# Negated row maxima carried in the query stack of an attention stage, in place of a product of their own

## The chip, the cores and the metric

One core of a Trainium2 chip runs the whole kernel in one launch. The metric is the device time of a launch in microseconds, the median of three runs. A profiled execution gives the trace; its own time stands beside its span below.

## The reference

A block of three parts over x of 8 batches x 256 tokens x 256 columns: a mixture-of-experts layer at half weight, attention, and the same experts again. The attention between them, on a layer-normed x, is

```python
q, k, v = (proj(w_q), proj(w_k), proj(w_v))          # 16 heads of 16
scores = jnp.einsum('bhqd,bhkd->bhqk', q, k) * SCALE
probs = jax.nn.softmax(scores, axis=-1)
attn = jnp.einsum('bhqk,bhkd->bhqd', probs, v)
return jnp.einsum('bsd,ed->bse', attn.transpose(0, 2, 1, 3).reshape(b, s, d), w_o)
```

## The kernel before, in words

The first stage routes the tokens and runs the first experts, the `attention` function does attention and the routing of the second experts, then come the second experts and the sum. Each engine has one program, written out by hand; semaphores tie them. `s_x` in the code is a semaphore, `wait_ge` waits for its count, `then_inc` counts at an instruction's end. DMAs count 16 at their landing.

**Split numbers.** TensorE multiplies in fp32r, so q and k are kept as a high and a low part. The two *stacks*, `qs` and `ks` (three buffers each, `NST`), hold for each of 8 head pairs 64 rows per head: row 4d + r of a half of the partitions is dim d in part r. The query stack has parts high, low, high, low and the key stack high, high, low, low, so that one 64-row matmul gives all four products of parts. `stack_heads` (L1291) fills row r of every four with one DMA of 256 KB from `qk`, issued on SyncE's queue (L1309 to L1314); for batch 0 ScalarE issues two of the key's.

**Attention, steps.** `cycle` (L1281) runs every engine's `step(b, j)` for b from -1 to 7 and j from 0 to 7; step j handles head pair j of batch b and, through `lagged` (L1287), the scores by key of the pair that is five steps (`LAG`) older: j = 5 has pair 0 of the same batch, j = 0 has pair 3 of the batch before.
- `scores` (L1453, TensorE): scores by query into `psS`; VectorE takes their negated maxima over the keys (`maximum`, L1723), one `tensor_reduce` of 1.2 us.
- After pairs 3 and 7, `split_maxima` (L1734) splits four pairs' maxima into high and low, TensorE's `maxima` (L1502) turns them (two transposes into `psG[1]`), and ScalarE's `maxima` (L1984) copies them to `nmT`: 8 rows per head parity (4 pairs high, then 4 low), 256 queries wide.
- `scores_by_key` (L1467): the pick product first, which adds to each score of pair j its query's negated maximum: `pick` is a matrix of zeros and ones that takes the high and low row of pair j out of `nmT`. Then the products of the stacks, keys by queries, on top of it. ScalarE takes the exponential of 1024 columns (`exponentials`, L1992), and `values` (L1487) multiplies by v.
- Between these stand projections of the next batch (`project`, `project_v`), the output's transposes and product (`by_query`, `by_dim`, `result`) and the routing of three batches before (`rows_turned`, `logits`, `ranks`, `gates_turned`, `biases`); GpSimd sums the partial results of the first experts (`sum_parts`, L1320) and sends routed rows by indirect DMA (`send`, L1350).

TensorE's `step` (L1610) has in step 0 scores, scores by key, `maxima(b - 1, 1)`, `rows_turned`, the projection of q; in step 4 scores, scores by key, `maxima(b, 0)`, `result`. ScalarE's `step` (L2072) has in steps 0 and 4 the exponential first, then the copy of the maxima. The maxima of the first half are first read in step 5, of the second half in step 1 of the next batch.

**SyncE in attention** (L1309): per batch, wait for the scores by key of batch b-3, load the partials of batch b+2 (1 MB), fill the query stack after `s_ql` (VectorE's low part of q, step 1 of the batch before), the key stack after `s_kl` (step 3).

**The pick table** is made in the first stage by GpSimd (`make_pick`, L183), between two inverse roots.

Of the kernel before, what the change touches and what calls it, by code (L numbers as in the profile page):

```python
# [14 lines left out]
P = 128  # L15
# [99 lines left out]
def constants(program, mem, x, x_in, nw, gate_wT, gate_b, b_raw):  # L115
# [20 lines left out]
    c["pick"] = mem.sb("pick", [P, NH // 4, P], fp32r)  # L136
    pick_f, picked = mem.sb("pick_f", [P, NH // 4, P], fp32), mem.sem("picked")
# [22 lines left out]
    def _(pool):  # L160
# [3 lines left out]
                  pool.memset(c["one_e"][:, :], 1.0), pool.memset(pick_f[:, :, :], 0.0)]  # L164
# [18 lines left out]
    def make_pick(pool):  # L183

        ch = Chain(pool, picked)
        for g in range(NH // 4):
            for line in (g, NH // 4 + g, P // 2 + g, P // 2 + NH // 4 + g):
                ch.link(pool.affine_select(out=pick_f[:, g, :], in_=pick_f[:, g, :], compare_op=ALU.not_equal, fill=1.0,
                                           base=-line, pattern=[[0, P]], channel_multiplier=1))
        ch.link(pool.tensor_copy(c["pick"][:, :, :], pick_f[:, :, :]))  # L190

# [4 lines left out]
    return c, (s_x_in, loaded, made, all_there, make_pick)  # L196
# [210 lines left out]
def route(program, nc, m, c, there, x, table, rows, banks, routed, split, b_raw, b_first, first_biases):  # L407
# [8 lines left out]
    s_x_in, loaded, made, all_there, make_pick = there  # L416
# [169 lines left out]
    def _(pool):  # L586
# [5 lines left out]
        make_pick(pool)  # L592
# [593 lines left out]
def attention(program, nc, m, c, x, xn, kbuf, proj, table, rows, psum, routed, early):  # L1186
# [24 lines left out]
    pick = c["pick"]  # L1211
# [57 lines left out]
    s_ld = [m.sem(f"ld{i}") for i in range(NST)]  # L1269
# [129 lines left out]
    def _(pe):  # L1399
# [53 lines left out]
        def scores(b, j):  # L1453
# [4 lines left out]
            if j == 0:  # L1458
                pe.wait_ge(s_ld[i], (b // NST + 1) * 128)
# [7 lines left out]
        def scores_by_key(b, j):  # L1467
# [3 lines left out]
            i, n, g = b % NST, b * HP + j, j % 4  # L1471
            pe.wait_ge(s_nT, n // 4 + 1)
# [5 lines left out]
            for odd in range(2):  # L1478
                rows = slice(odd * HALF, (odd + 1) * HALF)
                pe.matmul(bank[:, odd * 512:(odd + 1) * 512], pick[rows, g, :], nmT[rows, n // 4 % 2, None, :].to_broadcast([HALF, QT, S]), start=True, stop=False)  # L1480
            for k in range(QT):
                for odd in range(2):
                    rows = slice(odd * HALF, (odd + 1) * HALF)
                    last = pe.matmul(bank[:, (odd * QT + k) * S:(odd * QT + k + 1) * S], ks[i][rows, j, k * P:(k + 1) * P], qs[i][rows, j, :], start=False, stop=k == QT - 1)  # L1484
# [125 lines left out]
        def step(b, j):  # L1610
# [3 lines left out]
            scores(b, j)  # L1614
            scores_by_key(*lagged(b, j))
            if j == 0:
                maxima(b - 1, 1)
# [13 lines left out]
            if j == 4:  # L1631
                maxima(b, 0)
# [329 lines left out]
    def _(act):  # L1962
        def high_part(b, which):
# [7 lines left out]
            elif b > 0:  # L1971
                act.wait_ge(s_ld[(b - 1) % NST], 128 * ((b - 1) // NST + 1))
            act.activation(dst[0], src, ACT.Copy, scale=scale).then_inc(s_hi, 1)

        def keep_v(b):
# [3 lines left out]
            act.wait_ge(s_vz, 2)  # L1979
            since(act, s_pv, 4 * (b - 1))  # L1980
# [3 lines left out]
        def maxima(b, half):  # L1984
# [4 lines left out]
            since(act, s_t, 4 * (n - 1))  # L1989
# [82 lines left out]
        def step(b, j):  # L2072
            exponentials(*lagged(b, j))
            if j == 0:
                maxima(b - 1, 1)
# [7 lines left out]
            if j == 2:  # L2083
                high_part(b + 1, "k")
                if b < 0:
                    stack_heads(act, b + 1, "k", range(2, 4))
# [4 lines left out]
            if j == 4:  # L2091
                maxima(b, 0)
# [282 lines left out]
```

## Time and profile before

| | |
|---|---|
| median of 3 runs | 862.64 us (858.92 to 864.11) |
| profiled execution, its own time | 856.83 us |
| its span, first to last instruction | 855.1 us |
| attention stage in it | about 349 to 615 us |
| mean granted clock of TensorE in it | 0.957 |

In rows of a timeline: start in us, duration in us, engine, line, operation, what it writes <- what it reads, shapes, count of instructions merged into the row; in brackets the idle time of the engine before it and what ended that. In rows of groups: busy us, mean ns of one, then idle us before them by what ended it. SPq is SyncE's queue, PEld TensorE's weight loads. Names carry a prefix of their stage, `s_a_` for attention.

### The profile page before, as it was taken

The numbers are of one execution on the slowest core, as the hardware profiler recorded it, in microseconds if no ns is written. First come the engines' busy times: TensorE is split into PE (matmuls) and PEld (weight loads), VectorE is DVE, ScalarE is ACT, GpSimd is POOL, SyncE is SP. The second block draws the span as 40 slices with busy tenths as digits, with TensorE's granted clock in tenths as the row PEclk, the third lists the DMA queues.
The fourth block names the chain that finished last, engine by engine and source line by source line (L and its number), as shares of the span: only waits on it lengthen the run. The fifth ranks groups of instructions, "written<-read, shape, count | busy, mean of one in ns | idle before, by whom it ended". The sixth has DMA issues, their size and how long they took to land.

```text
span 855.1 us, 17528 instructions
## 1 busy us (share of the span) xinstructions
PE 729.3 (85%) x4774; PEld 568.2 (66%) x4774; DVE 602.2 (70%) x1435; ACT 432.6 (51%) x922; POOL 458.0 (54%) x446
## 2 busy tenths in 40 slices
PE   1775649999999997789999889787499999999984
PEld 1443326788888886667766667555268888888872
DVE  4775737777777776477787577457387777777766
ACT  3655324555555555257656455454325555555551
POOL 6876723666666667433344342146516666666672
PEclk9999999999999999999999798689689999999998
DMA  8998878868888753544453223027555787887766
GB/s 303 347 388 333 314 238 319 282 217 281 266 284 294 242 192 117 188 158 162 148 184 120 92 106 121 34 68 262 201 162 184 252 256 258 268 268 242 228 229 227
DMA packets 87419, 188.87 MB, mean 221 GB/s; under 512 B 13072, under 2 KB 37920, under 8 KB 85792
## 3 DMA queue, kind: packets, MB, share of 16 engines
q1 hardware_dynamic: 47104, 106.07, 36.4%
q10 hardware_dynamic: 26448, 41.92, 14.8%
q0 software_dynamic: 13776, 39.75, 12.2%
q8 instruction: 46, 0.75, 0.4%
q14 instruction: 45, 0.37, 0.1%
HBM read 105.46 MB, written 65.45 MB: 200 GB/s over the span
## 4 chain that ended last, share of the span: by engine, by line
PE 35%; DVE 13%; another core or an unknown queue 4%; issue 3%; ACT 2%; POOL 1%; DMA 0%; SPq 0%; DVEq 0%; ACTq 0%
PE s_psT L945 12%; PE s_psG L969 6%; DVE s_a_nm L1732 4%; PE s_psO L1499 3%; PE s_psS L1464 2%; PE s_psS L926 2%; PE s_psS L912 2%; PE s_psG L1436 2%; PE s_psT L1480 1%; DVE all_x L2188 1%; PE s_psT L1484 1%; PE s_psR L1571 1%; PE s_psG L1449 1%; PE s_psG L1522 1%
## 5 line engine op out<-in xcount | busy, mean ns | idle before, releaser
L1357 POOL DMA_INDIRECT rows<-s_a_row,s_a_slot_i x64 | 62.4, 975 | 107.6 <-DVE s_a_slot_i L1860 88.9
L1132 POOL DMA_INDIRECT kbuf<-s_e_own_ys,s_e_own_place x79 | 80.9, 1024 | 66.3 <-ACT s_e_own_ys L1078 58.3
L1132 POOL DMA_INDIRECT kbuf<-f_e_ys,f_e_place x79 | 80.9, 1024 | 66.3 <-ACT f_e_ys L1078 58.6
L945 PE MATMUL f_bank<-f_e_w,f_e_th 128*128 x316 | 114.3, 462 | 2.0 <-ACT f_e_th L1100 1.9
L945 PE MATMUL s_psT<-s_e_own_w,s_e_own_th 128*128 x316 | 112.1, 455 | 1.9 <-SPq L811 0.9
L1732 DVE TENSOR_REDUCE s_a_nm<-s_psS 128x4 f32<-128x1024 f32 x64 | 78.3, 1223 | 50.1 <-PE s_psS L1464 40.5
L1999 ACT ACTIVATE s_a_pT<-s_psT 128x1024 f32<-128x1024 f32 x62 | 63.4, 1022 | 47.0 <-PE s_psT L1484 30.4
L1008 DVE TENSOR_TENSOR s_e_own_hb<-s_psT,s_e_own_bias 128x512 f32<-128x512 f32 x79 | 54.5, 690 | 39.7 <-PE s_psT L945 38.7
L1008 DVE TENSOR_TENSOR f_e_hb<-f_bank,f_e_bias 128x512 f32<-128x512 f32 x79 | 54.5, 690 | 39.1 <-PE f_bank L945 37.2
L603 POOL DMA_INDIRECT rows<-f_r_row,f_r_slot_i x64 | 66.5, 1039 | 27.0 <-issue 18.5
L945 PEld LDWEIGHTS f_bank<-f_e_w,f_e_th 128*128 128x128 f32 x316 | 60.5, 192 | 22.5 <-issue 3.7
L945 PEld LDWEIGHTS s_psT<-s_e_own_w,s_e_own_th 128*128 128x128 f32 x316 | 59.4, 189 | 21.2 <-issue 2.5
L1138 POOL TENSOR_TENSOR f_e_bc<-f_e_bc,f_e_am 128x512 f32<-128x512 f32 x40 | 53.2, 1331 | 25.8 <-DVE f_e_bc L1041 24.9
L1138 POOL TENSOR_TENSOR s_e_own_bc<-s_e_own_bc,s_e_own_am 128x512 f32<-128x512 f32 x40 | 52.1, 1302 | 23.8 <-DVE s_e_own_bc L1041 22.6
L945 PE MATMUL f_bank<-f_e_w,f_e_tl 128*128 x158 | 56.3, 437 | 0.0
L945 PE MATMUL s_psT<-s_e_own_w,s_e_own_tl 128*128 x158 | 55.4, 431 | 0.0
L912 PE MATMUL f_bank<-all_ident,f_e_tb 128*128 128x128 f32 x160 | 43.4, 279 | 10.0 <-DMA f_e_tb<-rows 10.0
L969 PE MATMUL s_psG<-s_e_own_w,s_e_own_ah 128*128 x316 | 50.8, 283 | 0.2 <-issue 0.2
L969 PE MATMUL f_bank<-f_e_w,f_e_ah 128*128 x316 | 50.8, 282 | 0.1
L1078 ACT ACTIVATE s_e_own_ys<-s_psG,s_e_tb 128x256 f32<-128x256 f32 x79 | 37.5, 475 | 22.1 <-PE s_psG L969 21.3
L969 PEld LDWEIGHTS s_psG<-s_e_own_w,s_e_own_ah 128*128 128x128 f32 x316 | 45.6, 188 | 3.6 <-issue 0.4
L969 PEld LDWEIGHTS f_bank<-f_e_w,f_e_ah 128*128 128x128 f32 x316 | 45.6, 188 | 3.4 <-issue 0.3
(383 smaller groups left out, 1887.5 us busy)
## 6 DMA issues: line engine op xcount, KB each, us to landing
w_split<-stage ACTq DMA_DIRECT2D x10, 1536.0 KB
f_e_w<-w_split SPq DMA_DIRECT2D x24, 512.0 KB
s_e_own_w<-w_split SPq DMA_DIRECT2D x24, 512.0 KB
f_e_tb<-rows ACTq DMA_DIRECT2D x80, 144.0 KB
s_e_tb<-rows ACTq DMA_DIRECT2D x80, 144.0 KB
stage<-w_raw SPq DMA_DIRECT2D x11, 768.0 KB
s_a_qs<-s_a_qk SPq DMA_DIRECT2D x32, 256.0 KB, 2.5
s_a_ks<-s_a_qk SPq DMA_DIRECT2D x30, 256.0 KB, 2.5
```

Source lines behind the costliest of these rows:

```text
L603: pool.indirect_dma_start(out=rows[:, :], out_offset=bass.IndirectOffsetOnAxis(ap=slot_i[i][:, t, k:k + 1], axis=0), in_=row[i][:, t, :], ...
L912: last = pe.transpose(psT[:, j, k * P:(k + 1) * P], tb[:, (2 * p + j) % (2 * RING), k * P:(k + 1) * P], c["ident"][:, :])
L945: last = pe.matmul(psH[j][:, :], left[:, p % 2, j, k * P:(k + 1) * P], w1[:, bass.ds(buf, 1), h, k * I2:(k + 1) * I2], start=n == 0, stop= ...
L969: last = pe.matmul(psY[j][:, 0:D], left[:, p % 2, j, k * P:(k + 1) * P], w2[:, bass.ds(buf, 1), h, o:o + D], start=n == 0, stop=n == len(p ...
L1008: dve.tensor_tensor(hb[:, j, :], psH[j][:, :], bias[:, bass.ds(buf, 1), :].rearrange("p a n -> p (a n)"), ALU.add).then_inc(s_hb, 1)
L1078: act.activation(ys[:, n, :], psY[j][:, 0:D], ACT.Copy, scale=tb[:, slot, bass.ds(e + D, 1)]).then_inc(s_ys, 1)
L1132: pool.indirect_dma_start(out=kbuf[:, :], out_offset=bass.IndirectOffsetOnAxis(ap=place[:, n:n + 1], axis=0), in_=ys[:, n, :], in_offset=N ...
L1138: pool.tensor_tensor(bc[:, b, :, :], bc[:, b, :, :], am[:, b, :, :], ALU.mult).then_inc(s_u, 1)
L1357: pool.indirect_dma_start(out=rows[:, :], out_offset=bass.IndirectOffsetOnAxis(ap=slot_i[i][:, t, k:k + 1], axis=0), in_=row[i][:, t, :], ...
L1499: last = pe.matmul(bank[h * VW:(h + 1) * VW, :], vz[:, b % 2, k, 4 * q + h, :], pT[:, (4 * n + h) % 8, k, :], start=k == 0, stop=k == QT - 1)
L1732: dve.tensor_reduce(nm[:, b % 2, :, :, j].rearrange("p t o -> p o t"), src, X_AXIS, ALU.max, negate=True).then_inc(s_mx, 1)
L1999: act.activation(to, score_bank(n)[:, :], ACT.Exp).then_inc(s_e, 1)
```

## The change

The query and the key stack lose their fourth part (low by low). Row 3 of every four is zero instead, except two rows per half: rows 3 and 7, which hold the high and the low of the pair's negated maximum in the query stack and ones in the key stack. So the product of the stacks has the maximum in it, and the pick product, its table and `make_pick` go. Zeros come from the constant `pad`, ones from `vz` before its second half is written; ScalarE therefore waits for those DMAs before it first writes that half. While scores by query of a batch run, the rows of their pairs are still zero.

SyncE takes the rows from `nmT` into the query stack by two DMAs per half batch (`keep_maxima`): those of the first half behind the next batch's key stack, those of the second half at the head of the following round, ahead of the load of partials. Scores by key wait for them (`maxima_kept`) where they waited for ScalarE's copy; the copy waits for the DMAs of two halves before. From batch 3 on the two rows of a query stack are cleared again. TensorE turns the maxima ahead of the scores by key of steps 0 and 4, and ScalarE copies them ahead of the exponential.

```diff
@@ constants, route
-    c["pick"] = mem.sb("pick", [P, NH // 4, P], fp32r)
-    pick_f, picked = mem.sb("pick_f", [P, NH // 4, P], fp32), mem.sem("picked")
...
-        inverse_roots(0, GPT, 1)
-        make_pick(pool)
...
@@ attention
+    def stacked(engine, b):
+
+        engine.wait_ge(s_ld[b % NST], 16 * (4 + 6 + 8 * (b // NST)))
+
+    def key_rows_set(engine, i):
+
+        engine.wait_ge(s_set[i], 16 * 2)
+
+    def max_rows(stack, o):
+
+        return stack[o * HALF + 3:o * HALF + 8:4, :, :].rearrange("p g n -> p (g n)").bitcast(fp32)
+
+    def clear_maxima(queue, b):
+
+        i = b % NST
+        for o in range(2):
+            if b < NST:
+                queue.dma_start(qs[i][o * HALF + 3:(o + 1) * HALF:4, :, :].rearrange("p g n -> p (g n)").bitcast(fp32), c["pad"][:, 0:D]).then_inc(s_ld[i], 16)
+            else:
+                queue.dma_start(max_rows(qs[i], o), c["pad"][0:16, 0:D]).then_inc(s_ld[i], 16)
+
+    def clear_key_rows(queue, i):
+
+        for o in range(2):
+            queue.dma_start(ks[i][o * HALF + 11:(o + 1) * HALF:4, :, :].rearrange("p g n -> p (g n)").bitcast(fp32), c["pad"][0:112, 0:D]).then_inc(s_ld[i], 16)
+
+    def set_key_rows(queue, i):
+
+        for o in range(2):
+            queue.dma_start(max_rows(ks[i], o), vz[0:4, 1, :, :, :].rearrange("p t h w -> p (t h w)")).then_inc(s_set[i], 16)
+
+    def keep_maxima(queue, b, half):
+
+        n = 2 * b + half
+        queue.wait_ge(s_nT, n + 1)
+        for o in range(2):
+            to = qs[b % NST][o * HALF + 3:o * HALF + 8:4, 4 * half:4 * half + 4, :].rearrange("p g n -> p (g n)")
+            queue.dma_start(to.bitcast(fp32), nmT[o * HALF:o * HALF + 8, n % 2, :].bitcast(fp32)).then_inc(s_nq[n % 2], 16)
+
+    def maxima_kept(engine, n):
+
+        engine.wait_ge(s_nq[n % 2], 32 * (n // 2 + 1))
+
-    def stack_heads(queue, b, which, some=range(4)):
+    def stack_heads(queue, b, which, some=range(3)):
...
-        k, s_part, stack, parts = {"q": (0, s_ql, qs[i], (0, 1, 0, 1)), "k": (1, s_kl, ks[i], (0, 0, 1, 1))}[which]
+        k, s_part, stack, parts = {"q": (0, s_ql, qs[i], (0, 1, 0)), "k": (1, s_kl, ks[i], (0, 0, 1))}[which]
...
@@ sync
         for b in range(B):
+            if b >= 2:
+                keep_maxima(sp, b - 2, 1)
             since(sp, s_t, (b - NST + 1) * HP)
             if b + 2 < B:
                 load_parts(b + 2)
+            if b == 0:
+                clear_maxima(sp, 0)
+                clear_key_rows(sp, 0)
+                sp.wait_ge(s_vz, 2)
+                set_key_rows(sp, 0)
+            if b >= NST:
+                clear_maxima(sp, b)
             stack_heads(sp, b, "q")
-            stack_heads(sp, b, "k", range(2 if b == 0 else 4))
+            stack_heads(sp, b, "k", range(2 if b == 0 else 3))
+            if b == 0:
+                for i in range(1, NST):
+                    clear_maxima(sp, i)
+                    clear_key_rows(sp, i)
+                    set_key_rows(sp, i)
+            if b >= 1:
+                keep_maxima(sp, b - 1, 0)
+        keep_maxima(sp, B - 2, 1)
+        for half in range(2):
+            keep_maxima(sp, B - 1, half)
@@ tensor
             if j == 0:
-                pe.wait_ge(s_ld[i], (b // NST + 1) * 128)
+                stacked(pe, b)
+                if b < NST:
+                    key_rows_set(pe, b)
...
-            pe.wait_ge(s_nT, n // 4 + 1)
+            maxima_kept(pe, n // 4)
...
-            for odd in range(2):
-                rows = slice(odd * HALF, (odd + 1) * HALF)
-                pe.matmul(bank[:, odd * 512:(odd + 1) * 512], pick[rows, g, :], nmT[rows, n // 4 % 2, None, :].to_broadcast([HALF, QT, S]), start=True, stop=False)
...
             scores(b, j)
+            if j == 0:
+                maxima(b - 1, 1)
+            if j == 4:
+                maxima(b, 0)
             scores_by_key(*lagged(b, j))
...
@@ scalar
             act.wait_ge(s_nt, n + 1)
-            since(act, s_t, 4 * (n - 1))
+            if n >= 2:
+                maxima_kept(act, n - 2)
             act.activation(nmT[:, n % 2, :], psG[1][:, 0:S], ACT.Copy).then_inc(s_nT, 1)
...
+            if j == 0:
+                maxima(b - 1, 1)
+            if j == 4:
+                maxima(b, 0)
             exponentials(*lagged(b, j))
```

## Rows read from the trace of the kernel before

**Rows 1.** Page: busy us, share of the span and instructions of each engine

```profile
PE 729.3 (85%) x4774; PEld 568.2 (66%) x4774; DVE 602.2 (70%) x1435; ACT 432.6 (51%) x922; POOL 458.0 (54%) x446
```

**Rows 2.** Windows of batches 1, 4, 5: us, PE, PEld, DVE, ACT, POOL busy, PEclk, DMA share, GB/s

```profile
379.00:399.00 20.00, 18.88 (x202) 13.96 (x198) 14.72 (x28) 14.02 (x22) 5.64 (x4) 1.00 0.44 159
...
443.50:472.50 29.00, 25.17 (x239) 18.53 (x235) 21.32 (x60) 16.73 (x30) 14.51 (x13) 0.94 0.31 114
472.50:503.40 30.90, 27.23 (x239) 20.62 (x235) 21.43 (x61) 16.93 (x30) 9.62 (x10) 0.83 0.29 107
```

**Rows 3.** Timeline, first maxima of batches 2 and 4, steps 4 to 6

```profile
410.01 2.48 SPq L1298 DMA_DIRECT2D s_a_ks<-s_a_qk  x4
...
410.99 0.38 ACT L1990 ACTIVATE s_a_nmT<-s_psG 128x256 fp32r<-128x256 f32 x1
...
412.10 0.40 PE L1480 MATMUL s_psT<-s_a_nmT,all_pick 64*128 64x512 f32 x2
412.33 0.40 PE L1484 MATMUL s_psT<-s_a_qs,s_a_ks 64*128 64x256 f32 x4
...
415.45 0.50 PE L1464 MATMUL s_psS<-s_a_ks,s_a_qs 64*128 64x256 f32 x4
...
461.83 2.48 SPq L1298 DMA_DIRECT2D s_a_ks<-s_a_qk  x4
...
463.94 0.40 PE L1480 MATMUL s_psT<-s_a_nmT,all_pick 64*128 64x512 f32 x2
```

**Rows 4.** Timeline, second maxima of batch 2, steps 0 and 1 of batch 3

```profile
420.96 0.44 PE L1510 MATMUL s_psG<-all_ident,s_a_nmx 128*128 128x128 f32 x2
...
421.98 0.38 ACT L1990 ACTIVATE s_a_nmT<-s_psG 128x256 fp32r<-128x256 f32 x1
...
423.53 0.40 PE L1480 MATMUL s_psT<-s_a_nmT,all_pick 64*128 64x512 f32 x2
```

**Rows 5.** Timeline, second maxima of batch 4, the late signals

```profile
476.60 0.96 POOL L1357 DMA_INDIRECT rows<-s_a_row,s_a_slot_i  x1 [0.30 <-issue]
...
478.65 1.02 ACT L1999 ACTIVATE s_a_pT<-s_psT 128x1024 f32<-128x1024 f32 x1 [3.86 <-remote]
...
480.00 0.80 PE L1480 MATMUL s_psT<-s_a_nmT,all_pick 64*128 64x512 f32 x2 [2.40 <-ACT s_a_nmT L1990]
...
480.59 0.63 PE L1484 MATMUL s_psT<-s_a_qs,s_a_ks 64*128 64x256 f32 x4
```

**Rows 6.** Groups of instructions: scores, pick products, transposes of the maxima

```profile
L1464 PE MATMUL s_psS<-s_a_ks,s_a_qs 64*128 64x256 f32 x256 | 33.6, 342 | 12.7 <-DVE s_a_nm L1732 9.2 <-issue 3.3
...
L1480 PE MATMUL s_psT<-s_a_nmT,all_pick 64*128 64x512 f32 x124 | 28.4, 452 | 8.3 <-ACT s_a_nmT L1990 8.0 <-issue 0.2
...
L1510 PE MATMUL s_psG<-all_ident,s_a_nmx 128*128 128x128 f32 x32 | 6.9, 298 | 1.0 <-DVE s_a_at L1761 1.0
```

**Rows 7.** Landings by line: the stacks' 256 KB (L1298), partials' 1 MB (L1307), output stores (L2166)

```profile
DMA to landing us min/median/max: 2.3/2.5/4.4
...
DMA to landing us min/median/max: 5.3/5.4/5.6
...
DMA to landing us min/median/max: 2.0/2.6/3.5
```

**Rows 8.** Timeline, first maxima of batches 1 and 7, steps 4 and 5

```profile
389.72 2.48 SPq L1298 DMA_DIRECT2D s_a_ks<-s_a_qk  x4
...
391.29 0.39 PE L1480 MATMUL s_psT<-s_a_nmT,all_pick 64*128 64x512 f32 x2
...
554.92 0.38 ACT L1990 ACTIVATE s_a_nmT<-s_psG 128x256 fp32r<-128x256 f32 x1
...
556.02 0.40 PE L1480 MATMUL s_psT<-s_a_nmT,all_pick 64*128 64x512 f32 x2
```

**Rows 9.** Timeline, first stage, the second inverse root and its reader

```profile
14.32 2.28 POOL L590 TENSOR_TENSOR f_r_root<-f_r_var,all_minus_half 128x12 f32<-128x12 f32 x1
...
19.58 0.16 DVE L495 TENSOR_SCALAR f_r_gain<-f_r_root 128x6 f32<-128x6 f32 x1
```

More of the change, by code:

```diff
@@ L163, in _ @@
                   pool.memset(c["zero"][:, :], 0.0), pool.memset(c["spare"][:, :], 0.0), pool.memset(c["minus_half"][:, :], -0.5),
-                  pool.memset(c["one_e"][:, :], 1.0), pool.memset(pick_f[:, :, :], 0.0)]
+                  pool.memset(c["one_e"][:, :], 1.0)]
         for f in filled:
@@ L181, in _ @@
         pool.iota(c["places"][:, :, :], pattern=[[GPT * P, NG], [1, GPT]], base=-T, channel_multiplier=GPT, **approx).then_inc(made, 1)
[L183 to L190, printed above, removed]
     def all_there(engine, gates=True):
@@ L195, in all_there @@
         engine.wait_ge(made, 11 if gates else 10)
-    return c, (s_x_in, loaded, made, all_there, make_pick)
+    return c, (s_x_in, loaded, made, all_there)
 class Chain:
@@ L407, in route @@
 def route(program, nc, m, c, there, x, table, rows, banks, routed, split, b_raw, b_first, first_biases):
-    s_x_in, loaded, made, all_there, make_pick = there
+    s_x_in, loaded, made, all_there = there
     TT = NG * GPT
@@ L1210, in attention @@
     nmT = m.sb("nmT", [P, 2, S], fp32r)
-    pick = c["pick"]
     nmx = m.sb("nmx", [P, 2, QT, P], fp32)
@@ L1268, in attention @@
         "var", "rstd", "xn", "xT", "xh", "xl", "q", "qh", "ql", "k", "kh", "kl", "vp", "vv"))
-    s_ld = [m.sem(f"ld{i}") for i in range(NST)]
+    s_ld, s_nq = [m.sem(f"ld{i}") for i in range(NST)], [m.sem(f"nq{i}") for i in range(2)]
+    s_set = [m.sem(f"set{i}") for i in range(NST)]
     (s_s, s_mx, s_nh, s_nl, s_nt, s_nT, s_t, s_e, s_pv, s_o, s_on, s_rd, s_at, s_aT, s_ah, s_al, s_f, s_x) = (m.sem(n) for n in (
@@ L1470, in scores_by_key @@
                 return
-            i, n, g = b % NST, b * HP + j, j % 4
-            pe.wait_ge(s_nT, n // 4 + 1)
+            i, n = b % NST, b * HP + j
+            maxima_kept(pe, n // 4)
             bank = score_bank(n)
@@ L1483, in scores_by_key @@
                     rows = slice(odd * HALF, (odd + 1) * HALF)
-                    last = pe.matmul(bank[:, (odd * QT + k) * S:(odd * QT + k + 1) * S], ks[i][rows, j, k * P:(k + 1) * P], qs[i][rows, j, :], start=False, stop=k == QT - 1)
+                    last = pe.matmul(bank[:, (odd * QT + k) * S:(odd * QT + k + 1) * S], ks[i][rows, j, k * P:(k + 1) * P], qs[i][rows, j, :], start=True, stop=True)
             last.then_inc(s_t, 1)
@@ L1614, in step @@
             scores(b, j)
+            if j == 0:
+                maxima(b - 1, 1)
+            if j == 4:
+                maxima(b, 0)
             scores_by_key(*lagged(b, j))
             if j == 0:
-                maxima(b - 1, 1)
                 rows_turned(b - 3)
@@ L1631, in step @@
             if j == 4:
-                maxima(b, 0)
                 result(b - 2)
@@ L1971, in high_part @@
             elif b > 0:
-                act.wait_ge(s_ld[(b - 1) % NST], 128 * ((b - 1) // NST + 1))
+                stacked(act, b - 1)
             act.activation(dst[0], src, ACT.Copy, scale=scale).then_inc(s_hi, 1)
@@ L1979, in keep_v @@
             act.wait_ge(s_vz, 2)
+            if b == 1:
+                for n in range(NST):
+                    key_rows_set(act, n)
             since(act, s_pv, 4 * (b - 1))
@@ L2072, in step @@
         def step(b, j):
+            if j == 0:
+                maxima(b - 1, 1)
+            if j == 4:
+                maxima(b, 0)
             exponentials(*lagged(b, j))
             if j == 0:
-                maxima(b - 1, 1)
                 routed_turned(b - 3)
@@ L2085, in step @@
                 if b < 0:
-                    stack_heads(act, b + 1, "k", range(2, 4))
+                    stack_heads(act, b + 1, "k", range(2, 3))
                 routed_residual(b - 3)
@@ L2091, in step @@
             if j == 4:
-                maxima(b, 0)
                 if b >= 0:
```

## The prediction

> **What bounds the kernel now.** The profile page comes first, for scale: TensorE has records for 85% of the span, VectorE for 70% [rows 1]. Then the table of windows, cut at each batch's first scores. Batches 1, 4 and 5 of the attention stage take 20, 29.0 and 30.9 us. In batch 1 TensorE's records cover 18.9 us and VectorE has 5 to spare; in 4 and 5 TensorE has nearly 4 us without a record, and the clock is granted at 0.94 and 0.83 [rows 2]. So in the early batches the order written for TensorE sets the pace, and in the later ones a hole is added to it.
>
> The timeline shows the two places that the change touches. A batch has eight steps, and the scores by key run five steps later. The first maxima (heads 0 to 3) are turned in step 4 and first read in step 5; the second are turned in step 0 of the next batch and first read in its step 1. In batch 2 ScalarE's copy of the first ends at 410.99 + 0.38 = 411.37, and the pick product that reads it starts at 412.10: 0.7 us of slack [rows 3]. The copy of the second ends at 422.36 and is read at 423.53: 1.2 us [rows 4]. In batch 4 it is another picture: TensorE, idle for 2.40 us, reads the copy at 480.00, at the slow clock (the two picks take 0.80 where they took 0.40). ScalarE had waited to 478.65 for a signal that the view can't name, while GpSimd issued indirect DMAs one behind the other until 477.56 [rows 5]. Over the stage the wait for this copy is 8.0 us of TensorE's time [rows 6].
>
> **The change part by part.** All sums stand against the profiled execution: 856.83 us around a span of 855.1. It lies 5.8 us below the median of the three runs, 862.64; I come back to that at the end.
>
> *The pick products go.* Two 512-column matmuls in two row halves side by side: from the first pick to the first product is 412.33 - 412.10 = 0.23 us at the full clock [rows 3], 0.59 at the slow one [rows 5]. 64 steps x 0.23 = 14.7 us is the most at full clock. 16 of the steps are first reads, where the arrival of the maxima will set the start (below); they gain nothing. Of the other 48 (11.0 us) some gain nothing either, because the next scores wait for VectorE's maximum: 9.2 us of such waits today [rows 6]. I take 8, the slow clock's share included; bounds 5 and 15.
>
> *The low parts' products go.* They were row 3 of each four in the same 64-row matmuls, so no matmul gets shorter. Per batch SyncE has two copies of 256 KB fewer; four take it 2.48 us, so 0.62 each [rows 3].
>
> *The maxima take a DMA more.* This is the term that decides. After ScalarE's copy SyncE issues two small DMAs into the query stack, and TensorE waits for both. The trace has none like them. Nearest are the stack's own copies: 0.62 us to issue one, and 2.3 to 2.5 us from issue to landing, with 256 KB in each [rows 7]. Four follow at 0.62 us each and still land in 2.5, so at most 0.6 of that is bytes, which puts a small one between 2.3 - 0.6 = 1.7 and 2.5; the stores of the output land in 2.0 at best [rows 7]. I take 2.1, near those stores, and 0.5 for the issue ahead of it: 2.6 us from a free SyncE to both rows in place; bounds 2.1 and 3.2.
>
> "DMA: Bandwidth & Descriptors" of the Trainium skill (section Anatomy of one DMA) gives any DMA a fixed part of about 2.0 us, most of it the confirmation of the last write, with HBM the heaviest target. By it an estimate for this pair, which stays in SBUF, is 2.5 us at most, and the sum below would be 1 to 2 us less. The stores' row, to HBM, agrees at 2.0.
>
> *First half.* SyncE's program puts this pair behind the next batch's key stack. Those copies start at 410.01, when VectorE's low part is there, and three of them (one fewer than now) hold SyncE until 411.87; the maxima are ready at 411.4 or earlier and wait for it. 411.87 + 2.6 = 414.5 stands against a read at 412.10: 2.4 us. In batch 4, 461.83 + 1.86 + 2.6 = 466.3 against 463.94: 2.35 [rows 3]. In batch 1 the copies start at 389.72 and the read is at 391.29: 2.9. Batch 7 has no next stack: the copy ends at 555.30, some 0.6 earlier in the new order, and 554.7 + 2.6 = 557.3 stands against 556.02: 1.3 [rows 8]. Over eight batches 2 x 2.9 (batches 0, 1) + 5 x 2.35 + 1.3 = 18.9. Behind the waiting product on TensorE stand the values, a transpose and the 12 products that project v, and then the next scores, today at 415.45 [rows 3]. VectorE and ScalarE have one operation each in hand and run dry. Nothing fills the hole, so I count it whole.
>
> *Second half.* Here SyncE stands waiting, so only 2.6 us count, and the copy comes earlier: the transposes go ahead of one scores by key, the copy ahead of one exponential. Batch 2: transposes at about 420.5 in place of 420.96, copy done at 421.2, rows at 423.8 against 423.53: 0.3 [rows 4]. Where the signal comes late, ScalarE copies first, at 478.65, and is done at 479.05: rows at 481.65 against 480.00, 1.65 [rows 5]; 0.5 to 1.65, as TensorE now comes there later anyhow; I take 1.3 for each of the four late batches (3 to 6). Batches 0 and 1 have a read that follows the copy more closely, 0.9 each; the last, with a short tail behind it, 1.4: 1.8 + 0.3 + 5.2 + 1.4 = 8.7.
>
> *The transposes ahead.* They wait for VectorE's split and normalise, 1.0 us in all today with a scores-by-key group in front of them as cover [rows 6]. That group (0.23 us without its picks) now stands behind the wait: between 0 and 0.25 per half, 16 x 0.125 = 2.
>
> *The clock.* Waits of 2.3 to 2.9 us are new in TensorE. Batch 1 keeps the full clock with 1.1 us in all without a record [rows 2]; behind the 2.40 us before 480.00 it runs at half [rows 5]. Bounds: nothing, and the half clock behind each of eight waits. At half clock a step of about 2.5 us of TensorE work loses as much again: 8 x 2.5 = 20. I take 4: the wait is a single one, where the one before 480.00 had late signals ahead of it.
>
> *SyncE's other DMAs.* The load of partials for two batches on stood behind the key stack and now stands behind the second maxima, in batch 2 at about 422.5. It takes 5.4 us [rows 7], so GpSimd can sum from 428, and the statistics of it are due at the head of batch 4, 443.50 [rows 2]: cover 10 us even with a sum of 5, cost 0. The clears stand ahead of the query stack, which has six steps. In the prologue six small copies stand ahead of the first query stack, of which four overlap its wait; two cost 1 us, and two fewer stack copies give it back. The twelve behind delay only a load. 0, within 1 either way.
>
> *GpSimd's pick table goes.* Without it the second root of the first stage, at 14.32, could start up to 0.7 earlier. VectorE reads it at 19.58 only, behind its own queue [rows 9]: 3 us of cover, cost 0.
>
> Sum: -8 + 18.9 + 8.7 + 2 + 4 = +25.6; 856.8 + 25.6 = 882.4 for a profile like this one, and with a part of the 5.8 us to the median, 884.
>
> **The rivals.** (1) *Faster.* The small rows land in 1.7 us, SyncE issues them in 0.3, and the earlier transposes take away the 8.0 us of waiting; 14.7 + 8 = 23 of gain stands against first waits of 1.1 us, 8 x 1.1 = 9: 857 - 14 = 843. For it: 18.9 of 20 us in batch 1 are TensorE's. Against it: three key copies hold SyncE whatever a landing takes. (2) *Absorbed.* The waits of step 5 are had back in the later batches, because the late signals end with GpSimd's burst and not with TensorE's work: 5 x 2.35 = 11.8 less, and 5 less from the second half. 25.6 - 16.8 = +9: 866. Against it: the signals come one at a time there, so a step less is done when the burst ends. (3) *Slower still.* The clock falls behind every first wait, +16: 900. It fell in batches 4 and 5 [rows 2].
> That the change doesn't do what it says isn't likely to show in the time: the maxima must be in the stack before the read, whatever their values.
>
> **How the numbers follow.** Forecast 0.62, (1) 0.10, (2) 0.13, (3) 0.15. The forecast's own bounds: landing and issue move 15 waits by 0.5 each, -8 to +9, and the picks' gain is 5 to 15: 868 to 895. The range reaches into (2) and (3): 861 to 902. Faster 0.10 is (1); within 1% (854 to 871, about what a measurement of this kernel tells from no change) 0.12 is most of (2) and the forecast's edge; slower 0.78.
>
> **What would show it.** Right: the picks gone; in step 5 of every batch an idle TensorE of 2 to 3 us before the scores by key, ended by a DMA into the query stack; the row pair issued right behind three key copies; batch 1 at about 23 us where it was 20. The stages before and after unchanged within 1 us. Wrong: if step 5 shows no hole, I misread the landing or SyncE's order; if the hole is there and the batches aren't longer, something absorbed it, and I'd look in the stretch of late signals.

## The result and the profile after

| | before | after |
|---|---|---|
| median | 863.38 us (4 runs, 858.92 to 864.14) | 884.41 us (4 runs, 881.21 to 890.40) |
| ratio, 95% interval | | 1.027, 1.0226 to 1.0313: slower |
| profiled execution, its span | 856.83, 855.1 us | 890.40, 888.7 us |
| mean granted clock in it | 0.957 | 0.936 |

884.0 was forecast and 884.4 came out. A ratio with its interval is estimated from runs set beside one another; it isn't the quotient of the two medians (here 1.024) and can lie some tenths of a per cent from it. The profiled execution of after is the longest of its four, 6 us over their median, and that of before lies 6.5 us under its own. The two differ by 33.6 us where the medians differ by 21.0, so what they show is read as parts of a loss that is some 12.6 us too large.

The page's busy line and the group of the scores by key, of after; [rows 1] and [rows 6] are the ones of before that answer to them:

```profile
PE 737.0 (83%) x4646; PEld 569.4 (64%) x4646; DVE 607.5 (68%) x1435; ACT 433.2 (49%) x922; POOL 451.3 (51%) x428
...
L1533 PE MATMUL s_psT<-s_a_qs,s_a_ks 64*128 64x256 f32 x248 | 31.9, 340 | 22.4 <-DMA s_a_qs<-s_a_nmT 22.4
```

TensorE has 128 instructions fewer and is 7.7 us longer busy: the instructions that are left take longer, at a lower granted clock. The group shows the new wait: 22.4 us of an idle TensorE, ended by the maxima's DMA. The very last half is computed in another bank, `s_psS`, and waits 1.2 us more.

Batch 1 of after, step 4 to the scores of step 6, from the timeline:

```profile
399.11 0.41 PE L1559 MATMUL s_psG<-all_ident,s_a_nmx 128*128 128x128 f32 x2 [1.20 <-DVE s_a_at L1812]
...
399.55 0.38 ACT L2045 ACTIVATE s_a_nmT<-s_psG 128x256 fp32r<-128x256 f32 x1 [1.63 <-PE s_psG L1559]
399.58 1.82 SPq L1329 DMA_DIRECT2D s_a_ks<-s_a_qk  x3
400.82 0.50 PE L1516 MATMUL s_psS<-s_a_ks,s_a_qs 64*128 64x256 f32 x4 [0.86 <-DVE s_a_nm L1783]
401.45 1.36 SPq L1316 DMA_DIRECT2D s_a_qs<-s_a_nmT  x2
403.99 0.80 PE L1533 MATMUL s_psT<-s_a_qs,s_a_ks 64*128 64x256 f32 x4 [2.67 <-DMA s_a_qs<-s_a_nmT]
404.71 1.93 PE L1548 MATMUL s_psO<-s_a_pT,s_a_vz 128*32 128x256 f32 x16
...
406.92 2.91 PE L1499 MATMUL s_psG<-all_wp,s_a_xp 128*128 128x256 f32 x12
409.76 0.57 PE L1516 MATMUL s_psS<-s_a_ks,s_a_qs 64*128 64x256 f32 x4
```

The copy of the maxima is done at 399.93. SyncE issues the three key copies until 401.40, then the pair until 402.81; TensorE has the rows at 403.99, after 2.67 us of nothing. Behind the wait its work runs at half clock: the 16 value products take 1.93 us, the projection of v 2.91. The trace of the first experiment below, without the pair, has the same two at 1.07 and 1.68. Two shorter waits for VectorE, 1.20 and 0.86 us, stand ahead of the long one.

A hole of nearly the same kind in batch 4 leaves the clock alone. TensorE had no wait of 0.2 us or more in the 7 us ahead of it, and the value products behind it take their 1.07 us:

```profile
492.39 0.50 PE L1533 MATMUL s_psT<-s_a_qs,s_a_ks 64*128 64x256 f32 x4 [1.99 <-DMA s_a_qs<-s_a_nmT]
492.82 1.07 PE L1548 MATMUL s_psO<-s_a_pT,s_a_vz 128*32 128x256 f32 x16
```

Then the attention stage as a whole, from the first scores to the last scores by key, and batches 1, 4 and 5 in it. Windows: us, busy time of PE, PEld, DVE, ACT, POOL, PEclk, DMA share, GB/s. Before:

```profile
361.40:574.70 213.30, 189.57 (x1711) 138.80 (x1711) 148.99 (x372) 121.88 (x202) 74.14 (x67) 0.90 0.34 122
```

After:

```profile
362.20:605.40 243.20, 194.08 (x1582) 137.56 (x1583) 154.24 (x372) 122.53 (x201) 74.05 (x67) 0.84 0.28 97
...
387.60:413.90 26.30, 20.67 (x182) 14.27 (x182) 15.44 (x27) 14.00 (x21) 5.63 (x4) 0.87 0.28 102
467.90:500.50 32.60, 26.86 (x223) 19.69 (x219) 22.41 (x61) 16.88 (x30) 14.55 (x14) 0.84 0.33 120
500.50:531.90 31.40, 25.78 (x225) 19.04 (x221) 21.59 (x62) 16.77 (x30) 9.65 (x11) 0.89 0.25 92
```

The stage takes 29.9 of the 33.6 us by which the profiled executions differ. A window splits by one subtraction: length less PE busy is the time in which TensorE does nothing. Before it is 213.3 - 189.6 = 23.7 us, after 243.2 - 194.1 = 49.1: 25.4 us more. The batches lose unevenly: batch 1 has 26.3 us where it had 20.0, batch 4 has 32.6 where it had 29.0, batch 5 has 31.4 where it had 30.9 [rows 2].

Of the signs that the forecast named, the wait, what ends it and the order of SyncE's DMAs are there. Batch 1 takes 26.3 us and not about 23; the holes of step 5 lie between 1.15 and 5.62 us, not between 2 and 3, and the last batch has none; and behind the attention stage after is 2.9 us longer, not within 1.

### The profile page after: what moved, and what is told of

It reads as the page before. It is cut to its first block, busy times and chain, and to the rows that moved or that the text cites. A ratio compares the mean times of both kernels' runs of the same rounds, so it can differ in the third digit from the quotient of the medians.

```text
span 888.7 us, 17281 instructions
## 1 busy us (share of the span) xinstructions
PE 737.0 (83%) x4646; PEld 569.4 (64%) x4646; DVE 607.5 (68%) x1435; ACT 433.2 (49%) x922; POOL 451.3 (51%) x428
## 4 chain that ended last, share of the span: by engine, by line
PE 34%; DVE 10%; issue 4%; DMA 3%; another core or an unknown queue 3%; SPq 2%; POOL 2%; ACT 2%; ACTq 0%; DVEq 0%; POOLq 0%
PE s_psT L933 12%; PE s_psG L957 6%; DMA s_a_qs<-s_a_nmT 3%; DVE s_a_nm L1783 2%; PE s_psO L1548 2%; PE s_psS L900 2%; PE s_psS L914 2%; PE s_psS L1516 2%; PE s_psG L1486 2%; SPq L1329 1%; PE s_psG L1499 1%; PE s_psT L1533 1%; DVE all_x L2245 1%; SPq L1316 1%
## 5 line engine op out<-in xcount | busy, mean ns | idle before, releaser
L591 POOL DMA_INDIRECT rows<-f_r_row,f_r_slot_i x64 | 66.9, 1045 | 27.1 <-issue 18.5
L1126 POOL TENSOR_TENSOR f_e_bc<-f_e_bc,f_e_am 128x512 f32<-128x512 f32 x40 | 53.1, 1328 | 26.5 <-DVE f_e_bc L1029 25.6
L1126 POOL TENSOR_TENSOR s_e_own_bc<-s_e_own_bc,s_e_own_am 128x512 f32<-128x512 f32 x40 | 51.9, 1298 | 28.5 <-DVE s_e_own_bc L1029 27.3
L1533 PE MATMUL s_psT<-s_a_qs,s_a_ks 64*128 64x256 f32 x248 | 31.9, 340 | 22.4 <-DMA s_a_qs<-s_a_nmT 22.4
L1516 PE MATMUL s_psS<-s_a_ks,s_a_qs 64*128 64x256 f32 x256 | 35.5, 359 | 15.3 <-DVE s_a_nm L1783 15.3
```

Source lines behind the costliest of these rows:

```text
L591: pool.indirect_dma_start(out=rows[:, :], out_offset=bass.IndirectOffsetOnAxis(ap=slot_i[i][:, t, k:k + 1], axis=0), in_=row[i][:, t, :], ...
L1126: pool.tensor_tensor(bc[:, b, :, :], bc[:, b, :, :], am[:, b, :, :], ALU.mult).then_inc(s_u, 1)
L1516: last = pe.matmul(psS[:, (odd * QT + t) * S:(odd * QT + t + 1) * S], qs[i][rows, j, t * P:(t + 1) * P], ks[i][rows, j, :], start=True, st ...
```

## The experiments

Times are medians, and each ratio is against the kernel before, run beside the variant on the same chip: 862.0 us for e1 to e4, 863.1 for e5 to e7 (the same chip), 863.7 for e8 to e11 (a second chip), 811.8 for e12 (a third).

**e1: the change without its row DMAs.** It leaves out the subtraction of the maxima altogether.

```diff
-            if b >= 2:
-                keep_maxima(sp, b - 2, 1)
...
-            maxima_kept(pe, n // 4)
+            pe.wait_ge(s_nT, n // 4 + 1)
```

> The changed kernel without the 32 DMAs that take the negated maxima into the query stack; scores by key wait for ScalarE's copy alone, as before the change. It leaves out the subtraction of the maxima. Theory A (the DMA's issue and landing, and SyncE's order, are the cost): the 47 us of TensorE waits for these DMAs go, and what is left is the gain of the missing pick products and the prologue's clears: 845 to 862, at or below the kernel before. Theory B (the earlier transposes, or the prologue's clears and the later loads of partials, are the cost): 873 or more.

The 47 us in it add the waits of the weight loads to those of the matmuls behind them; they are the same holes, 22.4 us of them.

849.47 us (845.46 to 855.55), ratio 0.9845 (0.9774 to 0.9915). So the 32 small DMAs with all that waits for them cost 884.4 - 849.5 = 35 us, and the rest of the change is worth 12.5. The edit takes SyncE's waits for the maxima away too, and with them the delay of the loads of partials that stood behind; e10 below separates the two. The windows of its stage and its batch 1:

```profile
366.30:569.40 203.10, 175.55 (x1581) 124.25 (x1583) 149.54 (x372) 122.48 (x201) 74.03 (x67) 0.92 0.33 114
...
385.10:404.50 19.40, 17.68 (x184) 12.46 (x184) 14.58 (x27) 13.70 (x21) 5.63 (x4) 1.00 0.40 139
```

This is the ledger of the case. Against these rows the stage of after has 243.2 - 203.1 = 40.1 us more: 194.1 - 175.6 = 18.5 of the same instructions at a lower clock, and 49.1 - 27.6 = 21.6 of idleness, close to the 22.4 that the waits name. In batch 1 it is 6.9 us: 3.0 of lower clock (0.87 against 1.00) and 3.9 idle, of which the waits for the pair are 3.1.

**e2: the kernel before without its pick products.** It leaves out the same subtraction.

```diff
-            for odd in range(2):
-                rows = slice(odd * HALF, (odd + 1) * HALF)
-                pe.matmul(bank[:, odd * 512:(odd + 1) * 512], pick[rows, g, :], nmT[rows, n // 4 % 2, None, :].to_broadcast([HALF, QT, S]), start=True, stop=False)
...
```

> The kernel before without the 128 pick products, everything else as it was; it leaves out the subtraction of the maxima. My sum: 8 us faster (5 to 15), so 848 to 858. Rival: TensorE isn't the bound, its picks lie beside VectorE's waits, 0 to 3 us.

855.40 us (850.72 to 857.79), ratio 0.989 (0.9835 to 0.9944): 6.6 us, inside the forecast's 5 to 15.

**e3: the new order alone**, in the kernel before: transposes ahead of the scores by key on TensorE, the copy ahead of the exponential on ScalarE.

```diff
             scores(b, j)
+            if j == 0:
+                maxima(b - 1, 1)
+            if j == 4:
+                maxima(b, 0)
             scores_by_key(*lagged(b, j))
...
```

> The kernel before with only the order changed: transposes of the maxima ahead of the scores by key, ScalarE's copy ahead of the exponential. My sum: +2 (0 to 4). Rival (the earlier copy takes away the 8 us that TensorE waits for it in four places): 5 to 8 us faster.

858.32 us (854.04 to 864.24), ratio 0.9963 (0.9927 to 0.9999): 3.7 us less by the medians, with an interval that all but reaches 1, and no cost. In its trace no matmul waits for the copy of the maxima any more, and batches 5 and 6 take 27.6 and 27.4 us where they took 30.9 and 30.8; batches 0 to 4 are each 0.6 to 1.6 us longer.

**e4: the stacks alone**, in the kernel before: three parts, with the clears and the ones of the prologue. It leaves out the product of the low parts, as the change does.

```diff
-    def stack_heads(queue, b, which, some=range(4)):
+    def stack_heads(queue, b, which, some=range(3)):
...
+            if b == 0:
+                clear_maxima(sp, 0)
+                clear_key_rows(sp, 0)
+                sp.wait_ge(s_vz, 2)
+                set_key_rows(sp, 0)
```

> The kernel before with the change's stacks: three parts, the fourth row zero, ones in the key stack, with all clears in the prologue, picks and order as before. It leaves out the product of the low parts. My prediction said 0 (within 1). The trace of the changed kernel says that the partials' load behind twelve clears, at 368.5 in place of 358.8, piles 2.5 MB onto the queue: but here no small DMA waits behind it, so 0 to +3.

859.41 us (856.31 to 867.84), ratio 0.9978 (0.9939 to 1.0017): no difference that can be told.

**e5: the first half's pair ahead of the next key stack.**

```diff
+            if b >= 1:
+                keep_maxima(sp, b - 1, 0)
             stack_heads(sp, b, "k", range(2 if b == 0 else 3))
-            if b >= 1:
-                keep_maxima(sp, b - 1, 0)
```

> The changed kernel with the first half's pair of DMAs issued ahead of the next batch's key stack instead of behind it. Theory A: the pair then starts at ScalarE's copy and not 1.9 us behind VectorE's low part; each of seven waits in step 5 gets about 1.5 us shorter: 7 to 12 us faster than the changed kernel, 872 to 878. Rival (landing alone sets the wait, SyncE's order doesn't matter): within 3 us of 884.

886.66 us, ratio 1.0304 (1.0234 to 1.0374), with four runs from 876.23 to 891.54. The waits moved as expected (engine, line <- what ended the wait: us in all, times, the longest), here for the maxima's DMA:

```profile
PE s_psT L1533 <- DMA s_a_qs<-s_a_nmT: 14.5, 13, 3.1
```

The first half's holes fell from 2.67 and 1.99 us to 1.18 and 0.47, the stage of the profiled execution, which is the shortest of the four, from 243.2 to 232.5 us. The median didn't follow. Two of the four runs, 891.54 and 890.25 us, are some 10 us longer than the others, 876.23 and 883.08; the recorded ratio lies above what the two shorter ones alone would give. Theory A's 872 to 878 isn't confirmed, and I can't say whether the order is worth anything.

**e6: a mix.** The first head pair of each half keeps its pick product; only the other three take their maxima from rows, which gives the DMAs one more step of time. Old order of the transposes.

```diff
+            head = j % 4 < 1
+            if head:
+                pe.wait_ge(s_nT, n // 4 + 1)
+            else:
+                maxima_kept(pe, n // 4)
```

> The changed kernel with the pick product kept for the first pair of each half (16 of 64) and rows of the query stack for the other three, written a step later by four smaller DMAs; transposes and copy where they stood before the change; the first half's DMAs ahead of the key stack. Same result as the reference. Theory A: no first read waits for a DMA any more, so the loss goes whole: 48 x 0.23 of TensorE less than before, 850 to 862. Theory B (clears, loads, clock): 870 or more.

864.71 us (858.50 to 869.48), ratio 1.0018 (0.9983 to 1.0053). TensorE's waits for the DMA fall to 2.5 us in three, and the loss is gone. The gain over before that I expected from 48 saved pick products isn't there: the median lies between the ranges of the two theories.

**e7: matmuls on the identity ahead of the waits**, to keep TensorE busy, six and four rounds of them in the two first reads.

```diff
+            if j % 4 == 0 and n < B * HP - 4:
+                since(pe, s_e, n)
+                turn_over(pe, c, bank[:, 0:S], 6 if j == 0 else 4)
             maxima_kept(pe, n // 4)
```

> The changed kernel with idle TensorE kept at work while it waits: six extra 256-column products of the identity ahead of the wait in steps 5, four in steps 1, into the bank that the scores overwrite. Theory: the clock's fall behind the waits costs part of the loss (I had 4 us): the granted clock rises, 2 to 8 us faster than 884. Rival (the wait alone costs): 0, or slower where a fill outlasts the wait.

897.71 us (893.48 to 899.03), ratio 1.0402 (1.0342 to 1.0462): worse by 13. Batch 1, windows and timeline:

```profile
386.40:411.60 25.20, 22.66 (x204) 16.17 (x204) 15.50 (x27) 13.98 (x21) 5.66 (x4) 1.00 0.31 107
```

```profile
401.46 2.86 PE L217 MATMUL s_psT<-all_ident 128*128 128x256 f32 x12
404.25 0.50 PE L1536 MATMUL s_psT<-s_a_qs,s_a_ks 64*128 64x256 f32 x4
404.68 1.07 PE L1551 MATMUL s_psO<-s_a_pT,s_a_vz 128*32 128x256 f32 x16
...
405.87 1.68 PE L1499 MATMUL s_psG<-all_wp,s_a_xp 128*128 128x256 f32 x12
```

Where the filling covers the hole, the clock stays at 1.00, the step behind it is back at 1.07 and 1.68, and the batch takes 25.2 us where it took 26.3. So the half clock does come from the idleness. But the filling takes 2.86 us in a step 5 and 1.99 in a step 1 at full clock, and of after's holes only the first is longer; where a hole is shorter, the filling holds TensorE itself. Over the kernel that costs more than the clock gives.

**e8: order and stacks together**, in the kernel before (e3 and e4), to see whether the two small gains add up.

```diff
...
+            if j == 4:
+                maxima(b, 0)
...
-            stack_heads(sp, b, "k", range(2 if b == 0 else 4))
+            stack_heads(sp, b, "k", range(2 if b == 0 else 3))
```

> The kernel before with two parts of the change and without the maxima's DMAs: the transposes and ScalarE's copy of the maxima ahead of the scores by key, and stacks of three parts with their fourth rows cleared in the prologue (leaves out the product of the low parts, as the change does; the pick products stay). Theory A (the parts add up: -3.7 for the order, -2.6 for the stacks): 6 us under the kernel before of this job, 853 to 860. Rival B (both small gains are noise): 861 to 865, a ratio whose interval holds 1.

860.88 us (855.67 to 873.23), ratio 0.9979 (0.9951 to 1.0007). The two small gains don't add up: rival B, as far as an interval of 0.3% to either side can tell.

**e9: the mix of e6 with the new order**, in e6's own edit.

```diff
-            scores_by_key(*lagged(b, j))
             if j == 0:
                 maxima(b - 1, 1)
+            if j == 4:
+                maxima(b, 0)
+            scores_by_key(*lagged(b, j))
```

> As e6_mix (a pick product for the first head pair of each half, the maxima in rows for the other three, their DMAs ahead of the key stack), now with the transposes ahead of the scores by key as in the change. e6_mix stood at 864.7. Theory A (the order is worth 4 us wherever the maxima travel): 858 to 862. Rival B (behind a pick product the step has no cover left, so the order gains nothing): 863 to 867.

Ratio 1.0033 (0.9992 to 1.0075); its twelve runs lie from 859.69 to 878.61 with a median of 871.66, which is 1.009 of 863.67. By either number the order gains nothing here.

**e10: the loads of partials at their old place.**

```diff
+            if b == 0:
+                load_parts(2)
             if b >= 2:
                 keep_maxima(sp, b - 2, 1)
...
+            if b + 3 < B:
+                load_parts(b + 3)
```

> The changed kernel with SyncE's loads of partials issued at their old place: the first ahead of the clears, each later one behind the first half's row pair and ahead of the wait for the second half's. GpSimd waits 27 us for partials in the changed kernel and 1 in the one before. Theory A (GpSimd has that time to spare; the cost is TensorE's waits for the rows and what follows them): 880 to 888, but the first hole of 5.6 us falls to 3, so the lower part of that. Rival B (GpSimd's late sums are a part of the 12 us that the holes of TensorE do not account for): 868 to 877.

879.53 us (875.87 to 889.10), ratio 1.0157 (1.0108 to 1.0206): 1.1 points under the change's 1.027, about 10 us, with the two intervals apart by a little; the medians are only 4.9 us apart. It lies below theory A's range and above rival B's. GpSimd's wait for partials, of after:

```profile
POOL s_a_part L1374 <- DMA s_a_part<-kbuf: 27.2, 6, 8.7
```

and of e10, with TensorE's for the maxima and the window of its stage:

```profile
POOL s_a_part L1376 <- DMA s_a_part<-kbuf: 10.8, 2, 8.9
```

```profile
PE s_psT L1535 <- DMA s_a_qs<-s_a_nmT: 23.8, 14, 5.8
```

```profile
364.40:596.70 232.30, 184.17 (x1582) 129.04 (x1583) 149.91 (x372) 122.44 (x202) 74.00 (x67) 0.89 0.29 102
```

The waits for the DMA are all still there. What fell is PE busy, 194.1 to 184.2 us at a clock of 0.89 instead of 0.84. Part of that fall belongs to after's long profiled run, whose clock over the whole kernel, 0.936, is below the 0.943 to 0.948 of its other three. Set against e1, which has its loads in time as well (GpSimd waits 10.6 us there), e10 shows what the rows alone cost: a stage of 29.2 us more, of which 184.2 - 175.6 = 8.6 are lower clock and 48.1 - 27.6 = 20.5 idleness. The first hole stayed, at 5.84 us, where theory A had it fall to 3.

**e11: the pair issued by ScalarE** behind its own copy.

```diff
             act.activation(nmT[:, n % 2, :], psG[1][:, 0:S], ACT.Copy).then_inc(s_nT, 1)
+            keep_maxima(act, b, half)
```

> The changed kernel with all 32 row DMAs issued by ScalarE right behind its copy, not by SyncE. Theory A (the price is the time from the copy to the landing, wherever it is spent): the first half's holes fall by the time that SyncE held the pair (about 1.2 us each), ScalarE pays 1.2 us of issue per half, 16 x 1.2 = 19 us on an engine with slack in the early batches: 876 to 884. Rival B (ScalarE is late behind the issues, and the exponentials with it): 885 to 895. Rival C (the cost grows out of all proportion with a wait's length): 866 to 875.

878.74 us (875.35 to 883.75), ratio 1.0173 (1.0122 to 1.0224): in theory A's range, 6 us less by the medians and 8 by the ratios. The waits:

```profile
PE s_psT L1526 <- DMA s_a_qs<-s_a_nmT: 14.0, 10, 5.4
```

This edit frees SyncE of the pairs too, so the partials come in time as in e10 (GpSimd waits 11.0 us). It can't tell its two gains apart. Beside e10, 9.8 us less of these waits go with a median only 0.8 us lower; what takes the rest back wasn't tested.

**e12: e5 and e10 together.**

```diff
+            if b == 0:
+                load_parts(2)
...
+            if b >= 1:
+                keep_maxima(sp, b - 1, 0)
             stack_heads(sp, b, "k", range(2 if b == 0 else 3))
...
-            if b >= 1:
-                keep_maxima(sp, b - 1, 0)
+            if b + 3 < B:
+                load_parts(b + 3)
```

> The changed kernel with both of SyncE's orders mended: the first half's row pair ahead of the next key stack (e5) and the loads of partials at their old place (e10). e5 alone stood at 1.030 of the kernel before, e10 at 1.016, the change at 1.027. Theory A (what is left is the price of fetching 16 halves through a DMA at all: 0.65 us of issue and 1.8 of landing each, with the time lost around it): 870 to 876, a ratio of 1.008 to 1.015, still slower than before. Rival B (the orders were most of the loss): 862 to 867. Rival C (moving the pair ahead of the key stack gains nothing, as in e5): 877 to 882, as e10.

832.24 us (829.95 to 839.99) against 811.84 (808.52 to 815.29) for the kernel before on this other chip: ratio 1.0265 (1.0222 to 1.0308). None of the three theories said that. The waits, the first read of batch 1 in the timeline, and two windows, of batches 1 and 4:

```profile
PE s_psT L1535 <- DMA s_a_qs<-s_a_nmT: 11.2, 13, 3.5
```

```profile
391.96 0.51 PE L1535 MATMUL s_psT<-s_a_qs,s_a_ks 64*128 64x256 f32 x4 [1.18 <-DMA s_a_qs<-s_a_nmT]
392.40 1.81 PE L1550 MATMUL s_psO<-s_a_pT,s_a_vz 128*32 128x256 f32 x16
...
378.00:400.80 22.80, 19.58 (x182) 13.47 (x182) 14.42 (x27) 14.09 (x21) 5.65 (x4) 0.93 0.33 118
446.90:472.30 25.40, 22.67 (x223) 16.48 (x219) 21.54 (x61) 17.00 (x30) 14.53 (x14) 1.00 0.31 113
```

In the attention stage of this trace no wait is put down to the signals that the view can't name, which made up 34 us of waits in the stage of the kernel before, one of them in [rows 5], and 40 in after's. Batch 4 takes 25.4 us where before's takes 29.0 on the first chip, though it holds waits of the change. It may be that on the first chips the late signals hide a part of what the rows cost, and that here nothing does. That is a guess from one trace, not shown: the change itself and the kernel before weren't profiled on this chip, and of the 20.4 us only the 12.7 of waits for the DMA (11.2 and 1.5 more in another bank) are read from rows.

## Why the prediction was right

**The number is right, the sum behind it only in part.** The gain of the rest, the price of the clock and that of the loads of partials were forecast too small, the holes too large, and the errors nearly cancel. The last step was luck too: the +25.6 was added to an execution of 856.8 us, and only 1.6 of the 5.8 us up to the median went in. From the measured median of 863.4 the same sum gives 889, for a loss that was 21.0.

*The maxima's DMA, first half.* Forecast 18.9 us in holes of 2.9, 2.35 and 1.3. The trace has 5.62, then 2.67, 1.99, 1.15, 1.99, 1.98, 1.39, and none that names the DMA in the last batch: 16.8. SyncE's order is as read: three key copies, then the pair in all eight but the last. From the start of the pair's issue to TensorE's read batch 1 takes 403.99 - 401.45 = 2.54 us where 2.6 was taken. The two parts of that were wrong and cancel: an issue takes 0.61 to 0.70, where 0.5 was taken for all that is ahead of the second, and TensorE reads 1.8 behind the start of the second, where 2.1 was taken for its landing. The Trainium skill ("DMA: Bandwidth & Descriptors", Anatomy of one DMA) gives a fixed part of some 2.0 us, in a section on DMAs that GpSimd issues. These are SyncE's, and their 1.8, counted from the start of an issue, lies a little under it.

*The first hole.* 5.62 us instead of 2.9 (batch 0). Its pair is issued at 374.46 and read only at 379.59, 5.1 us later. The prologue had been priced at nothing, by its issues; the bytes of its clears, stacks and loads were not counted. That the pair lands behind them is likely, not shown, and which of them would hold it isn't settled: with the load moved ahead of the clears (e10) the hole is 5.84, from ScalarE's queue (e11) 5.37, and with the pair ahead of the key copies (e5) 3.12.

*Second half.* Forecast 8.7, found 0.44, 0.38, none, 1.31, 1.26, 1.26, 0.97 and, in the other bank, 1.2: 6.8 us. TensorE reads 2.4 to 2.5 us behind the copy's end, where 2.6 was forecast; in the early batches more of that was covered. With the first half 23.6 stand against 27.6.

*The clock.* This is the step that failed: "I take 4: the wait is a single one". By the ledger of e1 lower clock was worth 18.5 us in the profiled execution, the longest of four and with the loads delayed; by e10 against e1, with the loads in time in both, 8.6. Either is over twice the 4. The mechanism had been written down, with its bound: half clock behind a wait, and a step that loses as much again as it has work. In batch 1 the scores follow the read by 409.76 - 403.99 = 5.77 us, where before they followed by 415.45 - 412.33 = 3.12 [rows 3, batch 2]: 2.65, with 2.5 forecast for a step if the clock falls. Batch 1 has no late signal in it, so my reason against it, that late signals had to come first, fails there; it had one row behind it. e7 shows that the hole is needed: without it the same batch keeps 1.00. But the hole isn't all of it. In batch 1 waits of 1.20 and 0.86 us stand ahead of the 2.67. In e12 a hole of only 1.18 us, with one of 0.87 ahead, is followed by half clock (value products 1.81 us), while 1.99 us in batch 4 of after, behind steady work, is not (1.07 us). The hole of batch 2 is as long, 1.99 us with a wait of 0.56 ahead, and is followed by half clock (1.93 us). So the length of the one wait doesn't decide it; whether the waits ahead of it do wasn't tested.

*What the late batches absorb.* Batches 1 to 3 lose 6.3, 4.3 and 5.3 us by their first scores, batches 5 and 6 only 0.4 and 0.9, with holes of the same size. That looks like rival (2), but no absorption is needed. Without the rows (e1) batches 5 and 6 take 27.4 and 27.3 us, and against that after's lose 4.0 and 4.3, more than their holes of 3.2 and 2.7. e3 has the same 27.6 and 27.4 from the new order alone, where before took 30.9 and 30.8. So in these traces the order gains some 3.5 us in each of the two batches, and the rows take it back. These are single executions, and the medians of e3 and e8 show less of such a gain.

*The loads of partials.* Forecast 0 behind 10 us of cover. GpSimd waits 27.2 us for them where it waited 0.9: 1.6 and 8.7 in the prologue, where the clears delay the second load from 358.8 to 368.5, and 3.8 to 4.9 for each of the four later ones. e10 removes these four and gets 5 us back by the medians, 10 by the ratios. The cover itself was there: the load issued at 441.99 is being summed from 448.18, 20 us ahead of batch 4's first scores at 467.9. So it wasn't the statistics that came late, and the step that failed is to take GpSimd's wait for free because of them. e10's gain lies in a higher clock, not in fewer waits for the rows. How the load comes to lower the clock is open: TensorE's waits for VectorE's maxima fell from 15.3 to 11.7 us with it, which fits, and wasn't tested.

*The picks.* Forecast -8, -6.6 in e2. Once the order and the stacks are changed too they may be worth more: e1 lies 1.3 points under e8, 11.5 us. TensorE's busy time in the stage would allow it: 189.6 - 175.6 = 14.0, a part of which is clock (0.90 and 0.92).

*The order, the stacks, the pick table.* Forecast +2, 0 and 0. e8 holds all but the table and can't be told from no change, 0.9979; +2 for the order had the wrong sign if any. The table has no run of its own.

Put together by the medians: -12.5 for all but the rows and +35 for them, +22.5, beside the 21.0 between the two medians; -8, +2 and +31.6 (holes and clock) made +25.6 in the forecast. The two errors, 6.5 too little gain and 3.4 too little cost, pull opposite ways.

**The rivals.** (1) needed an issue of 0.3 and a landing of 1.7; the landing was near it, the issue twice as long. (2) isn't borne out, as above. (3) came true in part: the clock falls behind the first half's wait in batches 0 to 2, and stays up behind those of 1.15 to 1.99 us in batches 3 to 6.

**No version here beats both kernels beyond doubt.** The smallest ratio of a kernel that still subtracts the maxima is e3's, 0.9963, and e8, which holds its edit, doesn't confirm it.

## What to carry to other kernels

A copy through SBUF by DMA of even 8 KB, read by the engine that sets the pace, is a delay of about 2.5 us from a free queue to the first read; it has to be issued a whole step ahead of its reader, or the thing that it replaces (here 0.23 us of matmul per step) is cheaper; e6 did so and only broke even. Price a new hole in TensorE twice, once as the wait and once as the half clock of what may follow, the more so where other waits stand just ahead of it. When DMAs are put into a queue with waits of their own, look at what stands behind them, in the prologue too, and have an experiment that moves only that. And count a forecast from the same number that it will be held against, here the median and not the one profiled execution.

## What the runs showed of the hardware

The late signals of [rows 5] seem to belong to a chip or its moment, not to the kernel's text. In the traces from the first chips VectorE and ScalarE wait for signals that the view can't name, up to 5.5 us at a time in the stage of the kernel before; in the one trace from the last chip there is no such wait at all, its batches 4 and 5 took 25.4 and 25.2 us with a granted clock of 1.00, and the kernel before, not profiled there, took 811.8 us instead of 863. Six per cent between chips is more than twice what the change did, so only ratios from one chip say anything. The change's loss was as large there with its two orders mended, 2.65%, as on the first chip without.

TensorE's clock fell to half behind a wait of 1.18 us in one place (e12, batch 1, another of 0.87 ahead) and stayed at full behind one of 1.99 us in another (after, batch 4, steady work ahead). Filling the waits kept it at 1.00 in batch 1 (e7).
